# Quantised convolutions as four 64x64 tiles, with GpSimd in the quantisation: a residual chain of convolutions on one core

## The chip, the cores and the metric

One core of a Trainium2 chip runs the whole program. The metric is the device time of one execution in microseconds (us). The kernel before took 255.37 us (median of 3 runs, 255.18 to 255.53). What a profile shows is one execution, taken on its own.

## The reference

The input x is (16, 32, 28, 28) in float32. Four layers follow one another:

- Layer 0: a 1x1 convolution 32 to 192, a 3x3 convolution 192 to 192 and a 1x1 projection 192 to 32, all with ternarised weights, each with a batch norm, the first two with a clip to 0..6; then x is added.
- Layer 1: two 3x3 convolutions 32 to 32 with 8-bit quantised weights and activations. The input of each is scaled by 255 over the largest value of the **whole** tensor and rounded:

```
s = max(max(x), 1e-8) / 255;  q = clip(round(x / s), 0, 255) * s
out = relu(bn1(conv3x3(q(x), q(w1))))
out = relu(bn2(conv3x3(q(out), q(w2))) + identity)
```

- Layers 2 and 3: a 3x3 convolution 32 to 32, bias, batch norm, relu, and a channel of an image is set to zero if its largest value is under 0.001.

So layer 1 has two points at which everything waits for a maximum over all images: one ahead of each quantised convolution.

## The kernel before

**Layout.** The 16 images are taken four at a time: a chunk c (0 to 3) holds four images g in the four groups of 32 partitions, each with 32 channels, 784 pixels long. The final tensors y0, h1, yb have this layout, [128, 4, 784].

**Layer 0** runs through 16 images in `slot(c, g)` (L612 on TensorE, L937 on ScalarE, L1385 on VectorE). TensorE works as Winograd-like rows: `outer` (L561), `middle` (L550), `pair_middle` (L572), `pair_outer` (L583), and `expand_main`/`expand_rest` (L497, L514) for images further ahead. Once per chunk, in slot g = 0 of the next chunk, the 1x1 projection follows: `project(c, h)` (L594), twice, for the even and the odd rows (h = 0, 1). Each call has 8 matmuls of 128x32 tiles (128 rows, 32 columns of the array) on h2a and 8 of 64x32 tiles on h2b, whose half h lies in partitions 64h to 64h+63. VectorE reads the result in `residual(c, h)` (L1375), which adds x, writes y0 and takes the maximum. The last chunk's projection comes at the end of layer 0, and there the two halves signal apart. `expand_main(15, 0)` writes PSUM bank 6, which the projection of chunk 2 used, and so waits for `residual(2, 0)` (L508).

**Layer 1** (`step` L1553, `quant` L1561 and L1066, `qconv` L735). `step(k)` takes the maximum over all of it: VectorE reduces, TensorE spreads (`largest`, L729), VectorE reduces again and takes the reciprocal. Then, chunk by chunk: VectorE multiplies and adds a rounding constant (`quant`, L1566, into the two-buffer ra), ScalarE takes the constant off, clips at zero and casts to bf16 (L1069, into qi), TensorE does the convolution, ScalarE does relu and scale (`out1`, L1073), VectorE takes maxima (L1599). Each is cut into two halves of the rows. `qconv` uses a weight matrix wqi of 128x128 with four 32x32 blocks on its diagonal, one for each image of the chunk: 9 taps x 2 halves of 128x128 tiles, 18 matmuls a chunk, 72 for a convolution. Before the maxima and between them TensorE runs idle matmuls (`keep_warm`, L485).

After the second convolution, ScalarE has scaled and shifted the residual (`shifted`, L1091), and VectorE adds it to the result (`q_out`, L1646). Then VectorE splits the result into two float16 parts (`q_hi`, `q_lo`) and VectorE, ScalarE and DMAs copy these into stacks `kst` (`copies`, `stack`, `blocks`, `dup`) for layers 2 and 3, whose convolutions `lconv` (L758) use 128x32 tiles. The order on every engine is written out by hand: on VectorE from L1694, on TensorE from L790, on ScalarE from L1115, on the DMA queue from L401. The float16 weights of these convolutions are made on VectorE (L1575 to L1580) while the first quantised convolution runs; L1584 to L1589 are five small scalars beside it. GpSimd has only the set-up and, at the very end, three output scalings (L464).

Of the kernel before, what the change touches and what calls it, by code (L numbers as in the profile page):

```python
# [134 lines left out]
def conv_seq(nc, x, params, w1, w2a, w2b, w3, wq1, wq2, wc, wd, out):  # L135
    with ExitStack() as ctx:
# [322 lines left out]


# [7 lines left out]
        def _(pe):  # L468
# [125 lines left out]
            def project(c, h, steps=(0, 1, 2, 3), bank=7, end=False):  # L594

                if bank == 6 and not end:
                    pe.wait_ge(ra_ready, 2 * (G * (c + 1) + 2) + 2)
                wait(pe, y0_ready, (2 * c + h if end else 2 * c) if bank == 7 else 0)
                lower = slice(HB * h, HB * h + HB)
                for s in steps:  # L600
                    if s == 0:
                        pe.wait_ge(h2a_ready, (c + 1) * G + (h if end else 0))
                    if s == (2 if end else 1):
                        pe.wait_ge(h2_ready, (c + 1) * G)
                    for g in range(G):
                        w, rhs = ((w3t[:, 0, :], h2a[:, g, s, HALF * h:HALF * h + HALF]) if s < 2 else
                                  (w3t[lower, 1, :], h2b[lower, g, s - 2, :]))
                        i = nc.tensor.matmul(ps[C * g:C * g + C, bank, :HALF], w, rhs, start=(s == steps[0]),  # L608
                                             stop=(s == steps[-1]))
# [1179 lines left out]
```

## Time and profile before

| | |
|---|---|
| profiled execution | 254.96 us |
| its span, first to last instruction | 253.2 us |
| PE busy | 230.3 us (91%) |
| DVE (VectorE) busy | 226.3 us (89%) |
| ACT (ScalarE) busy | 178.6 us (71%) |
| POOL (GpSimd) busy | 8.7 us (3%) |
| mean granted TensorE clock | 0.999 |

Engine times are unions of the instructions of one engine; waiting is not in them. A matmul is shown with some 0.33 us although a new one can start 0.17 us after the last, so that a busy PE can hide small pauses. "idle before" is the engine's idle time, with the instruction that ended it.

### The profile page before, as it was taken

What the parts mean: (1) busy time and instruction counts of PE and PEld (TensorE: products, weight loads), DVE (VectorE), ACT (ScalarE), POOL (GpSimd) and SP (SyncE); (2) the same over time, 40 slices, a digit from 0 to 9 for tenths busy, and PEclk for the clock granted to TensorE, in tenths of its full rate; (3) what the DMA queues carried; (4) which work ended last, traced back from release to release, by engine and by line L of the source; (5) the groups of instructions that cost most, each with busy time, mean ns of one, the idle gap of its engine ahead of it and who ended that gap; (6) DMA issues with size and microseconds to landing.
All of it is one profiled execution on the core that took longest, in us unless ns stands there. A gap on an engine that the chain in (4) does not pass through costs nothing.

```text
span 253.2 us, 5577 instructions
## 1 busy us (share of the span) xinstructions
PE 230.3 (91%) x2151; PEld 132.2 (52%) x2151; DVE 226.3 (89%) x460; ACT 178.6 (71%) x268; POOL 8.7 (3%) x26
## 2 busy tenths in 40 slices
PE   0659998999999999999999999999979999789991
PEld 0315564556555555555555555465525555446551
DVE  3799999999999999999999997879777769999894
ACT  5899987885684586776376479683525739997963
POOL 4500000000000000000000000000000000000013
PEclk9999999999999999999999999999999999999999
DMA  7427202111003202003202001100000000264206
GB/s 234 119 58 242 61 1 70 28 28 38 0 21 84 58 3 63 1 3 87 74 0 57 11 0 34 32 3 0 3 1 1 3 0 12 54 153 104 61 20 254
DMA packets 9018, 13.13 MB, mean 52 GB/s; under 512 B 2560, under 2 KB 7136, under 8 KB 8992
## 3 DMA queue, kind: packets, MB, share of 16 engines
q1 hardware_dynamic: 8800, 12.74, 18.8%
q8 instruction: 17, 0.28, 0.5%
q14 instruction: 9, 0.07, 0.1%
q10 hardware_dynamic: 192, 0.04, 0.1%
HBM read 4.04 MB, written 1.61 MB: 22 GB/s over the span
## 4 chain that ended last, share of the span: by engine, by line
PE 68%; DVE 13%; DMA 5%; ACT 5%; SPq 3%; issue 3%; DVEq 0%; ACTq 0%
PE ps L556 17%; PE ps L567 17%; PE ps L589 10%; PE ps L578 8%; PE ps L742 5%; PE ps L608 2%; DMA big<-w2b_in 2%; PE ps L780 2%; PE ps L511 2%; SPq L390 2%; PE ps L677 2%; DVE big L1644 2%; DVE cmx L1689 2%; DMA big<-big 1%; DVE vv L1651 1%
## 5 line engine op out<-in xcount | busy, mean ns | idle before, releaser
L567 PE MATMUL ps<-vv,w2at 128*128 128x378 f16 (+1 forms) x192 | 37.2, 330 | 0.4 <-DVE ps L1330 0.4
L861 ACT ACTIVATE ra<-ps,bn 128x392 f32<-128x392 f32 x32 | 21.4, 676 | 22.9 <-PE ps L511 22.3
L556 PE MATMUL ps<-vv,wu 128*128 128x392 f16 x180 | 34.8, 329 | 0.1
L780 PE MATMUL ps<-big,wst 128*32 128x378 f16 (+10 forms) x576 | 24.5, 326 | 3.6 <-DVE big L1644 2.4
L567 PEld LDWEIGHTS ps<-vv,w2at 128*128 128x128 f16 x192 | 17.8, 98 | 15.3 <-issue 4.3
L742 PE MATMUL ps<-qi,wqi 128*128 128x378 bf16 (+7 forms) x144 | 23.9, 325 | 0.6 <-ACT qi L1069 0.6
L556 PEld LDWEIGHTS ps<-vv,wu 128*128 128x128 f16 x180 | 17.4, 98 | 12.1 <-DVE vv L1313 0.5
L780 PEld LDWEIGHTS ps<-big,wst 128*32 128x32 f16 x576 | 15.2, 96 | 13.0 <-issue 2.2
L567 PE MATMUL ps<-vv,w2bt 128*128 128x378 f16 (+1 forms) x96 | 21.2, 330 | 0.0
L556 PE MATMUL ps<-vv,wub 128*128 128x378 f16 (+1 forms) x90 | 19.9, 330 | 0.0
L742 PEld LDWEIGHTS ps<-qi,wqi 128*128 128x128 bf16 x144 | 13.8, 97 | 10.8 <-ACT qi L1069 1.4
L589 PE MATMUL ps<-vv,w2at 128*64 128x378 f16 (+1 forms) x192 | 19.0, 333 | 0.0
L893 ACT ACTIVATE hs<-ug,magic 128x784 f16<-128x784 f16 x16 | 15.1, 946 | 5.2 <-DVE ug L1273 5.1
L578 PE MATMUL ps<-vv,wu 128*64 128x378 f16 (+1 forms) x192 | 18.7, 330 | 0.0
L1330 DVE SCALAR_TENSOR_TENSOR ps<-ps,c1a 128x392 f32<-128x392 f32 x32 | 16.6, 563 | 2.3 <-ACT c1a L877 2.3
L913 ACT ACTIVATE r2a<-ps,bn 128x784 f32<-128x784 f32 x15 | 15.0, 1002 | 5.1 <-DVE h2a L1351 5.0
L870 ACT ACTIVATE ra<-ps,bn 128x392 f32<-128x392 f32 x18 | 12.0, 677 | 8.3 <-PE ps L526 8.3
L1100 ACT COPY big<-part 32x784 f16<-32x784 f16 x20 | 16.9, 843 | 1.0 <-DVE part L1683 0.7
L1287 DVE SCALAR_TENSOR_TENSOR hs<-ra,hs 128x784 f16<-128x784 f32 x16 | 15.4, 965 | 0.0
L1069 ACT ACTIVATE qi<-ra,magic 128x420 bf16<-128x420 f32 (+1 forms) x16 | 9.0, 611 | 9.0 <-DVE ra L1566 9.0
L1351 DVE SCALAR_TENSOR_TENSOR h2a<-r2a,h2a 128x784 f16<-128x784 f32 x15 | 14.5, 968 | 0.1
L589 PEld LDWEIGHTS ps<-vv,w2at 128*64 128x64 f16 x192 | 9.7, 109 | 8.1 <-issue 4.5
(220 smaller groups left out, 436.9 us busy)
## 6 DMA issues: line engine op xcount, KB each, us to landing
xk<-xpart SPq DMA_DIRECT2D x45, 49.0 KB, 1.9
xin<-x_in SPq DMA_DIRECT2D x4, 392.0 KB, 3.8
big<-part SPq DMA_DIRECT2D x25, 49.0 KB, 2.0
hs<-ug SPq DMA_DIRECT2D x12, 98.0 KB, 2.2
hs<-lowp SPq DMA_DIRECT2D x12, 98.0 KB, 2.2
big<-big SPq DMA_DIRECT2D x3, 392.0 KB, 3.6
y_out<-xin SPq DMA_DIRECT2D x3, 392.0 KB, 2.4
big<-w2a_in SPq DMA_DIRECT2D x3, 288.0 KB, 4.4
```

What stands on the lines that cost most here:

```text
L556: i = nc.tensor.matmul(landing(slice(0, P), PBANK[k], dx), weights(raw, mid, k, dx, False), moving(s, k, dx, b), start=(n == 0 and dx == D ...
L567: i = nc.tensor.matmul(landing(slice(0, P), PBANK[k], dx), weights(raw, mid, k, dx, False), moving(s, k, dx, b), start=False, stop=(n == 2 ...
L578: i = nc.tensor.matmul(landing(slice(HB * q, HB * q + HB), 4, dx), weights(raw, mid, k, dx, True), moving(s, k, dx, b), start=(n == 0 and ...
L589: i = nc.tensor.matmul(landing(slice(HB * q, HB * q + HB), bank, dx), weights(raw, mid, k, dx, True), moving(s, k, dx, b), start=False, st ...
L742: i = nc.tensor.matmul(img(ps[:, bank + h, :W * rows], rows)[:, to[0], to[1]], wqi[:, k, t, :], qi[:, c, of[0], of[1]], start=(t == TAP_OR ...
L780: i = nc.tensor.matmul(img(ps[C * g:C * g + C, bank + h, :W * n], n)[:, to[0], to[1]], wst[:, layer, C * t:C * t + C], kst[:, KBUF[layer][ ...
L861: nc.scalar.activation(ra[:, 0, HALF * h:HALF * h + HALF], ps[:, bank, :HALF], ACT.Relu, bias=bn[:, BSH, BN1A:BN1A + 1], scale=bn[:, BSC, ...
L893: nc.scalar.activation(rows_of(hs[:, MAIN_HI]), img(ug[:, 0, :]), ACT.Identity, bias=magic[:, 2:3]).then_inc(hha_ready, 1)
L913: nc.scalar.activation(img(r2a[:], 2), ps[:, 0:2, :HALF], ACT.Relu, bias=bn[:, BSH, BN2A:BN2A + 1], scale=bn[:, BSC, BN2A:BN2A + 1]).then_ ...
L1100: ins = nc.scalar.copy(kst[C * k:C * k + C, KBUF[layer][c], g], part[C * g:C * g + C, layer, c % 2, k])
L1287: stt(rows_of(hs[:, MAIN_LO]), img(ra[:, 0, :]), CAP, rows_of(hs[:, MAIN_HI]), ALU.min, ALU.subtract).then_inc(hla_ready, 1)
L1330: stt(ps[:, k, :HALF], ps[:, PBANK[2], :HALF], half, c1a[:], ALU.mult, ALU.add).then_inc(seed_a, 1)
```

## The change

- `qconv` no longer uses 128x128 tiles with a block diagonal of four images, but 64x64 tiles with a diagonal of two (wqi is half as wide). For each tap there are four matmuls: a pair of images (partitions 0 to 63, 64 to 127) by a half of the rows. Convolution 1 reads the pair from its partitions and writes the half `to` into partitions 64*half, so its output h1 has the half of the rows where the pair of images was, and the pair along the free axis. Convolution 2 reads that layout and writes the usual one. It needs a row of the other half at the seam, so its input is a new tile qh with a row above and below each half.
- The second step of the quantisation goes from ScalarE to GpSimd: `quant` for the first convolution, `quant_halves` for the second; ScalarE copies only the seam rows of qh (two small operations a chunk). `qconv` waits for both halves of a chunk. `shifted` goes to GpSimd as well, in a written order.
- `out1` is one ScalarE operation a chunk (two for the last), and one maximum each instead of two.
- `project` is one call for both halves: first the 128x32 tiles of both, then the 64x32 tiles of both, alternating between the upper and lower 64 rows of the array. It signals once, at its end, in the last chunk too.
- VectorE makes the weights of the later convolutions in the slots of the last chunk of layer 0 (`tail_weights`), and the five small scalars after them.
- On VectorE `quant(3, 1)` moves to a place between `q_hi(0)` and `q_lo(0)`. On TensorE the fourth chunk of convolution 2 moves ahead of `lconv(0, 0)`.

```diff
-            def project(c, h, steps=(0, 1, 2, 3), bank=7, end=False):
+            def project(c, banks, end=False):
...
+                wait(pe, y0_ready, 2 * c)
+                for h in range(2):
+                    pe.wait_ge(h2a_ready, (c + 1) * G + (h if end else 0))
+                    for s in range(2):
+                        for g in range(G):
+                            nc.tensor.matmul(ps[C * g:C * g + C, banks[h], :HALF], w3t[:, 0, :],
+                                             h2a[:, g, s, HALF * h:HALF * h + HALF], start=(s == 0), stop=False)
+                pe.wait_ge(h2_ready, (c + 1) * G)
+                for s in range(2):
+                    for k in range(G):
+                        for h in range(2):
+                            g = (k + 2 * h) % G
+                            lower = slice(HB * h, HB * h + HB)
+                            i = nc.tensor.matmul(ps[C * g:C * g + C, banks[h], :HALF], w3t[lower, 1, :],
+                                                 h2b[lower, g, s, :], start=False, stop=(s == 1))
                 i.then_inc(proj_done, 1)
...
             def qconv(k, c, bank, done):
...
+                for t in TAP_ORDER:
+                    for n in range(4):
+                        pair, half = n // 2, (n // 2 + n) % 2
+                        of, to = (pair, half) if k == 0 else (half, pair)
+                        out_, in_ = tap_window(t, HALF_ROWS * half, HALF_ROWS)
+                        lanes = slice(HB * of, HB * of + HB)
+                        if k == 0:
+                            moving_ = qi[lanes, c, in_[0], in_[1]]
+                        else:
+                            top = HALF_ROWS * half - 1
+                            moving_ = qh[lanes, c, pair, in_[0].start - top:in_[0].stop - top, in_[1]]
+                        i = nc.tensor.matmul(img(ps[HB * to:HB * to + HB, bank + of, :HALF], HALF_ROWS)[:, out_[0], out_[1]],
+                                             wqi[lanes, k, t, :], moving_, start=(t == TAP_ORDER[0]),
                                              stop=(t == TAP_ORDER[-1]))
-                    i.then_inc(done, 1)
+                i.then_inc(done, 1)
...
             for c in range(NCH):
-                wait(pe, h1_ready, 2 * (c - 1))
+                wait(pe, h1_ready, c - 1)
+                pe.wait_ge(q_ready, 2 * c + 2)
                 qconv(0, c, 2 * (c % 2), q1_done)
...
             def qconv2(c):
-                wait(pe, t1_ready, c - 1)
-                qconv(1, c, QBANK[c % 2], q2_done)
+                pe.wait_ge(qh_ready, c + 1)
+                pe.wait_ge(qm_ready, 2 * c + 2)
+                qconv(1, c, QBANK[c], q2_done)
```

On GpSimd:

```diff
+            def quant(c):
+                for h, rows in enumerate((slice(0, HALF_ROWS + 1), slice(HALF_ROWS + 1, H))):
+                    pool.wait_ge(q_v, 2 * c + h + 1)
+                    pts(qi[:, c, rows], img(qf[:, c % 2, :])[:, rows], -MAGIC, 0.0, ALU.add, ALU.max).then_inc(q_ready, 1)
+            def quant_halves(c):
+                for r in range(2):
+                    pool.wait_ge(q_v, 2 * (NCH + c) + r + 1)
+                    pts(qh[:, c, r, 1:HALF_ROWS + 1], img(qf[:, c % 2, HALF * r:HALF * r + HALF], HALF_ROWS), -MAGIC, 0.0,
+                        ALU.add, ALU.max).then_inc(qm_ready, 1)
+            def shifted(c):
+                pool.wait_ge(scale_ready, 2)
+                pts(y0[:, c, :], y0[:, c, :], col[:, BD + 2:BD + 3], col[:, SIG + 3:SIG + 4], ALU.mult,
+                    ALU.add).then_inc(ys_ready, 1)
+            for c in range(NCH):
+                quant(c)
+            quant_halves(0)
+            quant_halves(1)
+            shifted(0)
+            quant_halves(2)
+            shifted(1)
+            quant_halves(3)
+            shifted(2)
+            shifted(3)
```

On ScalarE, and then on VectorE:

```diff
+            def quant_halves(c):
+                act.wait_ge(q_v, 2 * (NCH + c) + 2)
+                nc.scalar.activation(qh[high_, c, :, 0], by_half[low, :, HALF_ROWS - 1], ACT.Relu, bias=magic[low, 0:1])
+                nc.scalar.activation(qh[low, c, :, HALF_ROWS + 1], by_half[high_, :, 0], ACT.Relu,
+                                     bias=magic[high_, 0:1]).then_inc(qh_ready, 1)
...
+            slot(NCH - 1, 0, last=True)
+            dve.wait_ge(ws_ready, 1)
+            tail_weights(0)
+            slot(NCH - 1, 1, last=True)
+            tail_weights(1)
+            slot(NCH - 1, 2, last=True)
...
             q_out(0)
             q_hi(0)
+            quant(3, 1, h1)
             q_lo(0)
```

## Rows read from the trace of the kernel before

**Rows 1.** Windows: us, busy time of PE, PEld, DVE, ACT, POOL; clock; DMA

```profile
60.00:100.00 40.00, 40.00 (x334) 22.87 (x333) 39.20 (x71) 27.04 (x41) 0.00 (x0) 1.00 0.15 37
...
220.00:230.00 10.00, 8.84 (x162) 5.17 (x154) 9.49 (x22) 8.91 (x12) 0.00 (x0) 1.00 0.56 127
...
252.00:253.20 1.20, 0.00 (x0) 0.00 (x0) 0.00 (x0) 0.00 (x0) 0.00 (x0) 0.72 0.19 72
```

**Rows 2.** Timeline, PE: projections; start, length, engine, line, tile, shape, count

```profile
159.96 0.52 PE L608 MATMUL ps<-h2a,w3t 128*32 128x392 f16 x8
160.40 0.51 PE L608 MATMUL ps<-h2b,w3t 64*32 64x392 f16 x8
...
161.74 1.17 PE L567 MATMUL ps<-vv,w2at 128*128 128x392 f16 x6
...
185.73 0.54 PE L608 MATMUL ps<-h2b,w3t 64*32 64x392 f16 x16
```

**Rows 3.** Timeline, DVE, last chunk of layer 0

```profile
161.59 0.62 DVE L1380 SCALAR_TENSOR_TENSOR y<-ps,bn,xin 128x392 f32<-128x392 f32 x1
...
170.07 1.05 DVE L1330 SCALAR_TENSOR_TENSOR ps<-ps,c1a 128x392 f32<-128x392 f32 x2 [1.00 <-ACT c1a L877]
...
180.11 0.64 DVE L1341 SCALAR_TENSOR_TENSOR ps<-ps,sgn,cy 128x392 f32<-128x392 f32 x1 [0.56 <-ACT cy L884]
```

**Rows 4.** Timeline, DVE: the weights that are moved

```profile
194.54 0.36 DVE L1577 TENSOR_SCALAR wcr<-wcr,col 128x288 f32<-128x288 f32 x1
...
195.77 0.37 DVE L1577 TENSOR_SCALAR wcr<-wcr,col 128x288 f32<-128x288 f32 x1
```

**Rows 5.** Timeline: end of layer 0

```profile
186.50 0.57 DVE L1363 SCALAR_TENSOR_TENSOR h2a<-r2a,h2a 128x392 f16<-128x392 f32 x1
...
187.26 0.63 DVE L1380 SCALAR_TENSOR_TENSOR y<-ps,bn,xin 128x392 f32<-128x392 f32 x1
```

**Rows 6.** Timeline: first quantised convolution

```profile
189.65 0.16 DVE L1555 TENSOR_REDUCE mx<-cmx 128x1 f32<-128x9 f32 x1
...
191.17 1.43 DVE L1566 TENSOR_SCALAR ra<-y,col 128x420 f32<-128x420 f32 x4
191.64 2.19 ACT L1069 ACTIVATE qi<-ra,magic 128x420 bf16<-128x420 f32 x4 [5.57 <-DVE ra L1566]
...
192.34 7.96 PE L742 MATMUL ps<-qi,wqi 128*128 128x392 bf16 x48 [0.27 <-ACT qi L1069]
```

**Rows 7.** Timeline: its end and the second maximum

```profile
201.31 0.68 ACT L1075 ACTIVATE h2a<-ps,bn,col 128x392 f32<-128x392 f32 x1 [0.66 <-PE ps L742]
202.02 0.56 DVE L1599 TENSOR_REDUCE cmx<-h2a 128x1 f32<-128x392 f32 x1 [0.78 <-ACT h2a L1075]
...
205.33 0.16 DVE L1555 TENSOR_REDUCE mx<-cmx 128x1 f32<-128x9 f32 x1
```

**Rows 8.** Groups by form, POOL: busy us, mean ns of one

```profile
L464 POOL TENSOR_SCALAR xin<-vv,keep 128x784 f32<-128x784 f32 x3 | 2.8, 918 | 236.4 <-DVE keep L1691 236.4
...
L455 POOL TENSOR_SCALAR bn<-bn 128x4 f32<-128x4 f32 x1 | 0.3, 254 | 0.1
```

**Rows 9.** Timeline: second quantisation up to the residual

```profile
208.91 1.41 DVE L1566 TENSOR_SCALAR ra<-h2a,col 128x420 f32<-128x420 f32 x4
...
211.54 1.03 DVE L1651 SCALAR_TENSOR_TENSOR vv<-ps,col,y 128x784 f32<-128x784 f32 x1 [0.25 <-ACT y L1092]
```

**Rows 10.** Timeline: two operations at one time in the set-up

```profile
7.24 0.96 DVE L1203 TENSOR_TENSOR xpart<-xrest 128x784 bf16<-128x784 f32 x1
7.77 0.49 POOL L449 TENSOR_TENSOR bn<-bn,par 128x9 f32<-128x9 f32 x1
...
8.61 0.20 POOL L453 TENSOR_TENSOR bn<-par,bn 128x9 f32<-128x9 f32 x1
```

**Rows 11.** Timeline, PE, after the second quantised convolution

```profile
218.41 3.10 PE L780 MATMUL ps<-big,wst 128*32 128x392 f16 x72 [1.46 <-DVE big L1644]
...
225.62 12.40 PE L780 MATMUL ps<-big,wst 128*32 128x392 f16 x288 [1.08 <-DMA big<-big]
```

More of the change, by code:

```diff
@@ L592, in pair_outer @@
                 i.then_inc(convb_done, 1)
-            def project(c, h, steps=(0, 1, 2, 3), bank=7, end=False):
-                if bank == 6 and not end:
+            def project(c, banks, end=False):
+                if not end:
                     pe.wait_ge(ra_ready, 2 * (G * (c + 1) + 2) + 2)
[L598 to L609, printed above, removed]
+                wait(pe, y0_ready, 2 * c)
[13 more added lines that the diff above has]
+                                                 h2b[lower, g, s, :], start=False, stop=(s == 1))
                 i.then_inc(proj_done, 1)
@@ L725, in _ @@
             pe.wait_ge(ra_ready, 2 * B)
-            project(NCH - 1, 0, end=True)
-            project(NCH - 1, 1, (2, 3, 0, 1), bank=6, end=True)
+            project(NCH - 1, (7, 6), end=True)
             def largest(n):
@@ L1076, in out1 @@
+            def out1(c):
+                act.wait_ge(q1_done, c + 1)
+                pieces = 1 if c < NCH - 1 else 2
+                for h in range(pieces):
+                    r = slice(h, h + 1) if pieces == 2 else slice(0, 2)
+                    bank = 2 * (c % 2)
+                    nc.scalar.activation(img(h1[:, c, :], 2)[:, r], ps[:, bank:bank + 2, :HALF][:, r], ACT.Relu,
                                          bias=bn[:, BSH, BNQ1:BNQ1 + 1],
                                          scale=col[:, SIG:SIG + 1]).then_inc(h1_ready, 1)
-            quant(0, 0)
@@ L1080, in _ @@
             act.wait_ge(scale_ready, 1)
-            for c in range(1, NCH):
-                quant(c, 0)
-                out1(c - 1)
-            out1(NCH - 1)
-            act.wait_ge(q1_done, 2 * NCH)
-            for c in range(2):
-                quant(c, 1)
-            act.wait_ge(scale_ready, 2)
-            def shifted(c):
-                nc.scalar.activation(y0[:, c, :], y0[:, c, :], ACT.Identity, bias=col[:, SIG + 3:SIG + 4],
-                                     scale=col[:, BD + 2:BD + 3]).then_inc(ys_ready, 1)
+            for c in range(NCH):
+                out1(c)
@@ L1095, in stack @@
+            for c in range(NCH):
+                quant_halves(c)
             def stack(layer, c):
@@ L1561, in quant @@
             def quant(c, k, src):
-                wait(dve, q_ready, 2 * (NCH * k + c - 1))
-                for px in (slice(0, HALF + W), slice(HALF + W, HW)):
+                if k and c >= 2:
+                    dve.wait_ge(qh_ready, c - 1)
+                    dve.wait_ge(qm_ready, 2 * (c - 1))
+                else:
+                    wait(dve, q_ready, 2 * (NCH * k + c - 1))
+                split = HALF if k else HALF + W
+                for px in (slice(0, split), slice(split, HW)):
                     ts(qf[:, c % 2, px], src[:, c, px], c1(RS + k), MAGIC, ALU.mult, ALU.add).then_inc(q_v, 1)
@@ L1614, in _ @@
             quant(1, 1, h1)
-            for c in range(2, NCH):
-                quant(c, 1, h1)
+            quant(2, 1, h1)
             def halves_l(layer, c):
```

98 lines of the change are left out of this document (37 added, 61 removed).

## The prediction

> **What bounds the kernel now.** Read the windows first. In layer 0 TensorE is busy all 40.00 of 40 us while VectorE has 39.20; in the last part (220 to 230 us) VectorE has 9.49 of 10 us and TensorE 8.84 [rows 1]. So there are three regimes: layer 0 goes by TensorE, with VectorE close behind; the two maxima of layer 1 are a chain in which each engine waits for the next; the splitting and stacking afterwards goes by VectorE. Then the timeline, engine by engine, at the places the diff touches: what a freed engine is worth depends on the regime.
>
> I write "before" for the profiled execution: 254.96 us, span 253.2. It lies 0.4 us under the median of 255.37, which I add at the end.
>
> **Projections in layer 0.** The two calls start at 159.96 and the next work at 161.74: 1.78 us. The step from one shape of tile to another is visible: 0.44 us from 159.96 to 160.40 for two passes of 0.17, thus 0.1 more [rows 2]. Can 64-row tiles in the upper and lower half run at one time? At 185.73, 16 matmuls of 64x32 took 0.54 us where 8 took 0.51: yes [rows 2]. The new order has four passes of 128x32 and two of eight 64x32 tiles, with two changes of shape: 6 x 0.17 + 2 x 0.1 = 1.2 us. 0.57 us less for each of three projections. For chunks 0 and 1 that is 1.1 us on the engine that bounds; bounds: 0, if VectorE (39.20 of 40) can't follow, and 1.7 with the third.
>
> **Weights moved into the last chunk.** One `tail_weights` takes 1.2 us of VectorE (start to start, 194.54 to 195.77) [rows 4]. The first delays `residual(2, 0)` from 161.59 to 162.8, done 163.45. TensorE needs bank 6 of it for `expand_main(15, 0)`, nine matmuls after 161.74, that is at 163.24, and with the faster projection at 162.67: it now waits, the third gain is gone and 0.2 us more. VectorE then idles 1.0 us ahead of L1330 at 170.07 and 0.56 us ahead of 180.11 [rows 3], which hides most of both; the second one and the five scalars (0.7 us, at 0.15 each from start to start) come through with some 0.3 us. I take +0.5; bounds -0.6 (all hidden, third gain kept) and +1.9 (nothing of 2.5 us hidden but the 0.57).
>
> **Last projection.** Before, `residual(3, 0)` started 0.76 us after L1363 started and waited for no matmul [rows 5]. Now it waits for the common signal: L1363 ends at 187.07, then two passes of 128x32, a change, two of 64x32 and 0.33 us of latency: about 188.1 instead of 187.26: +0.8. Bounds +0.3 and +1.0.
>
> **First quantised convolution**, from L1555 to the next L1555: before 205.33 - 189.65 = 15.7 us [rows 6, 7]. GpSimd's price: 918 ns for 784 elements and 254 for 4 [rows 8] make 0.25 us + 0.85 ns an element: 0.61 and 0.56 us for the two halves, 1.17 a chunk. ScalarE needed 2.19 us for four, 1.10 a chunk [rows 6], so the rate is no loss. But the convolution now waits for both halves: VectorE's first at 191.17, GpSimd from +0.57 (0.47 was ScalarE's, 0.1 is my guess for GpSimd's later start) to +1.74, TensorE at +1.8 instead of +1.17.
> Then the matmuls: 48 in 7.96 us, so 0.162 us each, 2.92 a chunk [rows 6]. Four 64x64 tiles at one time need nine passes: 1.46. TensorE chunks start at +1.8, 3.3, 4.7, 6.2, and the last ends at +7.8; GpSimd delivers at +1.7, 2.9, 4.1, 5.25, always in time. After that two ScalarE operations of 0.68 and a maximum of 0.56 [rows 7] put L1555 at +9.7. From L1555 to L1555: 1.52 + 9.7 = 11.2 us, a gain of 4.5, if GpSimd and VectorE don't touch each other.
>
> **Do they?** In the set-up a GpSimd operation on 128x9 took 0.49 us beside a two-input VectorE operation and ended 0.06 us after it; the like, alone, took 0.20 [rows 10]. So one row says that GpSimd waits for VectorE. The multiplications L1566 (four of 420 elements in 1.43 us, under 1 ns an element, so two elements at a time [rows 6]) are followed at once by GpSimd. If each GpSimd operation and each VectorE operation take turns, eight of 0.585 and eight of 0.35 make 7.5 us, TensorE's last chunk starts at +7.5 instead of +6.2, and the gain is 3.2. An operation has a dispatch part that needs no memory, so turns cost less than their sum; I take half: gain 3.9. Bounds: 4.5 and, if the tiles don't overlap, a loss of 1.3 (below).
>
> The Trainium skill (SBUF — State Buffer, "Who interferes with whom") speaks against the change: VectorE in a two-port mode or with two SBUF inputs and GpSimd hold the shared port pair exclusively, and "the other fully blocks". Row and rule agree for the wait of GpSimd; no row here shows VectorE held up by GpSimd. By the rule in both directions the result is the second case below.
>
> **Second quantisation.** Before, from L1555 to `q_out(0)` 6.2 us [rows 7, 9], held by ScalarE's `shifted(0)`. Now GpSimd does quant_halves(0), then (1), which has to wait for the second multiplication, 208.91 - 205.33 = 3.6 us after L1555 [rows 7, 9], and then `shifted(0)`: 3.6 + 0.57 + 1.17 + 0.92 = 6.3. So the double speed of TensorE buys nothing here: the wait is for the residual as before. With turns between the engines +0.5; bounds 0.06 and +2.0 (small scalars of VectorE held up by two GpSimd operations, 1.1, and three later turns). ScalarE's seams (two operations, under 0.55 each) lie beside GpSimd's 1.17.
>
> **After that** VectorE has no pause, and its work is the same, except that `quant(3, 1)`, which stood in the wait for `shifted(0)`, stands now between q_hi and q_lo: +0.7 (half of 1.41 [rows 9]). `shifted(1)` can be late for `q_out(1)`: +0.3; bounds 0 and +2.7 (after `shifted(0)` GpSimd has four operations of 0.58 and three of 0.92, 5.1 us, and about half of that can meet q_hi, quant(3), q_lo and the copies). ScalarE loses some 8 us of work here, worth nothing: VectorE bounds.
>
> **Sum:** -1.1 + 0.5 + 0.8 - 3.9 + 0.5 + 0.7 + 0.3 = -2.2. 254.96 - 2.2 = 252.8, and 0.4 to the median: **253.2 us**.
>
> **The rivals.**
> 1. *No conflict at all:* -1.1 + 0.5 + 0.8 - 4.5 + 0.1 + 0.7 = -3.5: 251.9 us. For it: the GpSimd operations at the end took 918 ns beside VectorE maxima, but those read a single input. It belongs to my forecast's own range, 251.5 to 254.6.
> 2. *Exclusive in both directions (the slower side).* VectorE's multiplications, scalars, q_hi, q_lo and copies wait for whole GpSimd operations: -1.1 + 0.5 + 0.8 - 3.2 + 2.0 + 0.7 + 2.7 = +2.4: 257.8 us. It decides once VectorE loses over 2.2 us after the second maximum, beyond the forecast. For it rows 10; against it that a small wait of GpSimd was seen, none of VectorE.
> 3. *The tiles don't overlap as 64x64.* Then the first stage has 4 x 2.92 behind +1.8, ends its last maximum at +15.5, 17.0 in all, +1.3 instead of -3.9; sum +3.0: 258.4. Against it: both kinds of overlap exist in the trace, column tiles (72 in 3.10 us [rows 11]) and row tiles [rows 2].
> 4. *The clock falls.* TensorE's fourth chunk used to lie in the pause between 221.5 and 225.62 [rows 11]; now the pause is empty, 4.1 us. At the end TensorE stops at 248.1, and in 252.0 to 253.2 the granted clock is 0.72 [rows 1]: full until about 252.5, so 4.4 us after the last matmul it fell to half (1.2 GHz). If it falls here, the 3.1 us of `lconv(0, 1)` and part of the next take twice as long and VectorE waits for the result: +2: 255.2.
>
> **Chances.** Forecast with rival 1: 0.55 (of it 0.15 near 252). Rival 2: 0.24. Rival 3: 0.06. Rival 4: 0.15, half of it inside "same", the rest on both sides. A measurement of this kernel tells 0.2%, 0.5 us, from no change: faster means under 254.9, slower over 255.9. Faster 0.60, same 0.12, slower 0.28. Range 251.3 to 257.7, which leaves out half of rival 2's upper side and rival 3.
>
> **What would show it.** L742's successor at 36 matmuls in about 1.5 us a chunk (rival 3: 2.9). Mean duration of the GpSimd operations: 0.58 and 0.61 if free, more if they wait; multiplications at 0.35 or stretched; q_lo at 0.97 or more. L1555 to its successor: 11.2 to 12.5 us. `q_out(0)` released by GpSimd. Granted clock in the pause before `lconv(0, 1)`. The projection at 1.2 us. The forecast is wrong if VectorE's operations beside GpSimd are stretched by over 2 us in all, or if layer 0 ends later than before.

## The result, and the profile after

The changed kernel takes **264.76 us** (median of 4 runs, 264.63 to 267.21) against 255.31 us (4 runs, 255.18 to 255.53): ratio 1.0388, 95% interval 1.0361 to 1.0416. The forecast was 253.2, its range ended at 257.7. The profiled execution took 264.63 us, its span is 262.8. Of the page, busy times and the chain that ended last:

```profile
PE 224.3 (85%) x2295; PEld 130.4 (50%) x2295; DVE 228.9 (87%) x457; ACT 168.2 (64%) x253; POOL 38.3 (15%) x47
...
PE 52%; DVE 19%; POOL 10%; ACT 8%; issue 5%; DMA 3%; SPq 2%; DVEq 0%; ACTq 0%
```

VectorE's 226.3 us became 228.9, TensorE's 230.3 became 224.3, ScalarE lost 10.4; GpSimd went from 8.7 to 38.3 us, and it is a tenth of the chain. The windows show where (columns as in [rows 1]):

```profile
190.00:200.00 10.00, 6.94 (x84) 3.96 (x84) 5.34 (x18) 1.00 (x1) 8.00 (x6) 0.83 0.00 0
...
210.00:220.00 10.00, 6.15 (x73) 3.72 (x72) 6.29 (x19) 2.16 (x7) 10.00 (x7) 0.66 0.01 2
220.00:230.00 10.00, 6.54 (x116) 4.27 (x120) 8.64 (x12) 4.76 (x7) 7.65 (x6) 0.83 0.16 42
```

In 210 to 220 us GpSimd (the last of the five engines in a row) is busy all ten microseconds, the other three stand idle for part of them (TensorE has 6.15, VectorE 6.29, ScalarE 2.16), and the granted clock is 0.66. GpSimd's groups by form (busy us, mean ns):

```profile
L470 POOL TENSOR_SCALAR qh<-ra 128x392 bf16<-128x392 f32 x8 | 13.0, 1647 | 5.7 <-DVE ra L1616 5.7
L464 POOL TENSOR_SCALAR qi<-ra 128x420 bf16<-128x420 f32 x4 | 6.5, 1638 | 182.2 <-DVE ra L1616 182.2
L464 POOL TENSOR_SCALAR qi<-ra 128x364 bf16<-128x364 f32 x4 | 5.7, 1420 | 0.0
L476 POOL TENSOR_SCALAR y<-y,col 128x784 f32<-128x784 f32 x4 | 5.0, 1247 | 0.0
```

The quantisation takes 1.42 to 1.65 us where I had put 0.56 to 0.61. In the first stage TensorE does its chunks quickly and waits for them (timeline, PE; what answers to [rows 6] on L742). The first row holds two chunks, with the granted clock at 0.50 in 196 to 198 us:

```profile
195.18 4.82 PE L779 MATMUL ps<-qi,wqi 64*64 64x392 bf16 x72 [2.80 <-POOL qi L464]
201.21 1.66 PE L779 MATMUL ps<-qi,wqi 64*64 64x392 bf16 x36 [1.21 <-POOL qi L464]
204.18 1.66 PE L779 MATMUL ps<-qi,wqi 64*64 64x392 bf16 x36 [1.31 <-POOL qi L464]
```

On VectorE (what answers to [rows 6, 7, 9]) the two maxima, `q_out(0)` and what follows it:

```profile
189.96 0.16 DVE L1601 TENSOR_REDUCE mx<-cmx 128x1 f32<-128x9 f32 x1
...
207.76 0.16 DVE L1601 TENSOR_REDUCE mx<-cmx 128x1 f32<-128x9 f32 x1
...
217.12 1.03 DVE L1683 SCALAR_TENSOR_TENSOR vv<-ps,col,y 128x784 f32<-128x784 f32 x1 [3.03 <-POOL y L476]
218.19 0.73 DVE L1689 TENSOR_SCALAR part<-vv 128x784 f16<-128x784 f32 x1
218.84 0.99 DVE L1616 TENSOR_SCALAR ra<-h2a,col 128x392 f32<-128x392 f32 x2
...
220.76 1.05 DVE L1663 COPY big<-part 32x784 f16<-32x784 f16 x1
...
226.77 1.03 DVE L1683 SCALAR_TENSOR_TENSOR vv<-ps,col,y 128x784 f32<-128x784 f32 x1 [0.97 <-POOL y L476]
```

These starts cut any variant of the kernel into four stretches. The table has them for all, each from its own timeline; "before" is the kernel before, "after" the changed one. A row is one execution: that of 7 is the fastest of its ten (255.31 us, median 257.77), that of 12 the slowest of its five (253.30, median 252.20).

| span in us | to max 1 | max 1 to max 2 | max 2 to q_out(0) | q_out(0) to end | span |
|---|---|---|---|---|---|
| before | 189.65 | 15.68 | 6.22 | 41.62 | 253.2 |
| after | 189.96 | 17.80 | 9.36 | 45.72 | 262.8 |
| 1 quantisation on ScalarE | 190.07 | 12.55 | 7.06 | 44.72 | 254.4 |
| 2 the same, idle matmuls | 189.82 | 12.55 | 7.06 | 43.09 | 252.5 |
| 3 before, quantisation on GpSimd | 189.91 | 18.78 | 9.10 | 41.86 | 259.6 |
| 4 before, new projection | 189.30 | 15.68 | 6.23 | 41.60 | 252.8 |
| 5 fast form in conv 2 only | 190.64 | 17.81 | 7.02 | 47.10 | 262.6 |
| 6 the same, idle matmuls | 190.08 | 17.81 | 7.02 | 43.86 | 258.8 |
| 7 add,mult everywhere, no clip | 189.66 | 11.26 | 7.03 | 45.56 | 253.5 |
| 8 steps exchanged, idle matmuls | 190.14 | 12.06 | 7.13 | 43.27 | 252.6 |
| 9 as 2, residual on GpSimd | 189.83 | 12.55 | 5.52 | 44.05 | 252.0 |
| 10 as 9, quant(3, 1) later | 190.00 | 12.55 | 5.52 | 43.64 | 251.7 |
| 11 as 10, gated | 189.84 | 12.55 | 5.52 | 43.64 | 251.5 |
| 12 as 11, fewer idle matmuls | 191.14 | 12.55 | 5.52 | 42.29 | 251.5 |

The first column doesn't tell small differences: variants with the changed kernel's layer 0 have 189.66 to 191.14 there, and the kernel before has 189.65 here and 190.30 and 191.08 in the executions of the two benches.

### The profile page after: what moved, and what is told of

Read it like the earlier page. It is cut to its first block, busy times and chain, and to the rows that moved or that the text cites. A ratio compares the mean times of both kernels' runs of the same rounds, so it can differ in the third digit from the quotient of the medians.

```text
span 262.8 us, 5871 instructions
## 1 busy us (share of the span) xinstructions
PE 224.3 (85%) x2295; PEld 130.4 (50%) x2295; DVE 228.9 (87%) x457; ACT 168.2 (64%) x253; POOL 38.3 (15%) x47
## 4 chain that ended last, share of the span: by engine, by line
PE 52%; DVE 19%; POOL 10%; ACT 8%; issue 5%; DMA 3%; SPq 2%; DVEq 0%; ACTq 0%
PE ps L596 14%; PE ps L585 13%; PE ps L607 7%; PE ps L618 7%; POOL qh L470 5%; POOL qi L464 5%; DMA big<-w2b_in 2%; PE ps L540 2%; PE ps L708 2%; PE ps L779 2%; PE ps L818 2%; DVE cmx L1721 1%; ACT big L1134 1%; PE ps L725 1%; DVE big L1676 1%
## 5 line engine op out<-in xcount | busy, mean ns | idle before, releaser
L464 POOL TENSOR_SCALAR qi<-ra 128x420 bf16<-128x420 f32 (+1 forms) x8 | 12.0, 1529 | 182.2 <-DVE ra L1616 182.2
L818 PE MATMUL ps<-big,wst 128*32 128x378 f16 (+10 forms) x576 | 25.2, 333 | 5.2 <-DMA big<-big 4.4
L585 PEld LDWEIGHTS ps<-vv,wu 128*128 128x128 f16 x180 | 17.4, 98 | 11.8 <-DVE vv L1342 0.2
L779 PE MATMUL ps<-qh,wqi 64*64 64x378 bf16 (+2 forms) x144 | 10.1, 447 | 7.3 <-POOL qh L470 7.3
L1145 ACT ACTIVATE vv<-ps,bn,col 128x392 f32<-128x392 f32 (+2 forms) x16 | 10.3, 676 | 9.3 <-PE ps L818 9.2
L1119 ACT ACTIVATE h2a<-ps,bn,col 128x784 f32<-128x784 f32 (+1 forms) x5 | 4.3, 872 | 17.4 <-PE ps L779 17.4
```

Source lines behind the costliest of these rows:

```text
L464: pts(qi[:, c, rows], img(qf[:, c % 2, :])[:, rows], -MAGIC, 0.0, ALU.add, ALU.max).then_inc(q_ready, 1)
L585: i = nc.tensor.matmul(landing(slice(0, P), PBANK[k], dx), weights(raw, mid, k, dx, False), moving(s, k, dx, b), start=(n == 0 and dx == D ...
L779: i = nc.tensor.matmul(img(ps[HB * to:HB * to + HB, bank + of, :HALF], HALF_ROWS)[:, out_[0], out_[1]], wqi[lanes, k, t, :], moving_, star ...
L818: i = nc.tensor.matmul(img(ps[C * g:C * g + C, bank + h, :W * n], n)[:, to[0], to[1]], wst[:, layer, C * t:C * t + C], kst[:, KBUF[layer][ ...
```

## The experiments

"x us beside y" gives the medians of the variant and of the kernel before, measured together; then come their ratio and its 95% interval.

**What a GpSimd operation costs by its form.** My theory after the result: the form `add, max` is slow. Rivals: the bf16 output, or VectorE beside it.

```diff
  (in words) forms on GpSimd at the end of the kernel before, then four times more beside VectorE operations
+ (qd, src, -MAGIC, 0.0, ALU.add, ALU.max), (y0, ...same), (qd, src, -MAGIC, 1.0, ALU.add, ALU.mult), (y0, ...same),
+ (y0, src, 1.0, 1.0, ALU.mult, ALU.mult), (qd, src, -MAGIC, ALU.add), (qd, src, 0.0, ALU.max), (784: mult, add by columns)
```

> The kernel before, and after its last computation GpSimd runs eight forms of tensor_scalar one after another, first with VectorE idle, then four times more beside VectorE operations: 14 multiplications of 784 float32 (two elements at a time), 14 additions with two SBUF inputs, 14 maxima, 14 float16 copies. The extra work changes no output. In the changed kernel GpSimd's operation on 392 elements took 1.51 us where I had 0.58. Theory 1 (the form): the operation with a maximum in it is slow by itself: 1.5 us with VectorE idle, while mult,mult and add,mult on the same 392 elements take about 0.6, whatever the output type. Theory 2 (the output type): bf16 output is what is slow; then add,mult into bf16 takes 1.5 and add,max into float32 0.6. Theory 3 (contention): with VectorE idle all forms take about 0.6 and only beside the multiplications, additions and copies 1.5. In all of them the residual form (mult,add with two column scalars, 784 elements) should take 0.95 alone and up to 1.7 beside two-port or two-input VectorE work, but not beside maxima.

Timeline, POOL, with VectorE idle: add,max into bf16, into float32; add,mult into bf16; add alone; mult,add on 784:

```profile
250.93 1.56 POOL L487 TENSOR_SCALAR qi<-ra 128x392 bf16<-128x392 f32 x1 [1.00 <-ACT xin L1163]
252.58 1.52 POOL L487 TENSOR_SCALAR y<-ra 128x392 f32<-128x392 f32 x1
254.18 0.52 POOL L487 TENSOR_SCALAR qi<-ra 128x392 bf16<-128x392 f32 x1
...
255.98 1.20 POOL L487 TENSOR_SCALAR qi<-ra 128x392 bf16<-128x392 f32 x1
...
258.55 0.99 POOL L487 TENSOR_SCALAR y<-ra,col 128x784 f32<-128x784 f32 x1
```

Beside single-input float32 operations of VectorE the first and the third of them:

```profile
259.91 2.15 POOL L487 TENSOR_SCALAR qi<-ra 128x392 bf16<-128x392 f32 x1 [0.21 <-DVE cmx L1772]
...
264.31 0.71 POOL L487 TENSOR_SCALAR qi<-ra 128x392 bf16<-128x392 f32 x1
```

The form decides, a factor of three; the output type doesn't matter. VectorE beside it costs 0.2 to 0.6 us on top, and is itself stretched: 0.57 to 0.75 us where one alone takes 0.56. VectorE's rows beside that first one:

```profile
259.74 0.56 DVE L1775 TENSOR_SCALAR r2a<-ra 128x784 f32<-128x784 f32 x1 [9.17 <-issue]
...
260.34 2.92 DVE L1775 TENSOR_SCALAR r2a<-ra 128x784 f32<-128x784 f32 x4
```

Beside VectorE additions with two SBUF inputs `add, max` took 2.22, `add, mult` 1.12 and the scaling of 784 elements 1.78 instead of 0.99. Beside VectorE reductions neither engine changed (1.53 and 0.97), beside float16 copies only VectorE did (0.36 to 0.56). A second bench asked which operation is slow; I had come to it by experiment 5 below, where `add, add` was slow too.

```diff
  (in words) the forms of the first bench exchanged for others
- add,max; add,mult; mult,mult; add; max; on 784: mult,add
+ add,add; add,mult; mult,add; mult,max; max,mult; mult; on 784: add,max; add,mult
```

> The kernel before with eight more GpSimd operations appended at its end (its total time means nothing), once with VectorE idle and once beside single-input VectorE operations. Single arithmetic forms on 128x392 float32 into bf16: add,add; add,mult; mult,add; mult,max; max,mult; mult alone; and on 128x784 into float32 add,max and add,mult. If a multiplication among the two operations makes the form fast (theory F), then add,add takes about 1.5 us, mult alone, add,mult, mult,add, mult,max and max,mult all about 0.52, and at 784 elements add,max about 2.7 and add,mult about 1.0. If max is slow in itself beside add,add (theory G), mult,max and max,mult take 1.2 us or more. If a single operation is slow whatever it is, mult alone takes 1.2 us.

The first five in this order, and `add, max` on 784 elements:

```profile
251.70 1.55 POOL L487 TENSOR_SCALAR qi<-ra 128x392 bf16<-128x392 f32 x1 [1.00 <-ACT xin L1163]
253.34 0.52 POOL L487 TENSOR_SCALAR qi<-ra 128x392 bf16<-128x392 f32 x1
253.94 0.52 POOL L487 TENSOR_SCALAR qi<-ra 128x392 bf16<-128x392 f32 x1
254.54 1.55 POOL L487 TENSOR_SCALAR qi<-ra 128x392 bf16<-128x392 f32 x1
256.17 1.53 POOL L487 TENSOR_SCALAR qi<-ra 128x392 bf16<-128x392 f32 x1
...
259.07 2.84 POOL L487 TENSOR_SCALAR y<-ra 128x784 f32<-128x784 f32 x1
```

Neither theory holds in full: a multiplication alone took 1.20, and one paired with a maximum 1.53 to 1.55. Fast were only the pairs add,mult, mult,add and mult,mult; the rest took 1.20 to 1.56 us, the pair add,max 3.4 ns an element ((2.84 - 1.52)/392, both into float32).

**The complement: everything but GpSimd (1), and GpSimd alone (3).**

```diff
 1, on ScalarE instead of GpSimd, in the new layout
+ nc.scalar.activation(qi[:, c, rows], ..., ACT.Relu, bias=magic[:, 0:1]).then_inc(q_ready, 1)   # and qh, and the residual
 3, in the kernel before: its quantisation's second step only
+ pts(qi[:, c, rows], ..., -MAGIC, 0.0, ALU.add, ALU.max).then_inc(q_ready, 1)
```

> The changed kernel with everything kept (64x64 tiles, new projection, moved weights) except that both quantisation steps' second half and the residual scaling are back on ScalarE, GpSimd has none of it. If the loss of 9.4 us is GpSimd's price: maximum to maximum (L1601) about 12 us instead of 17.8 (ScalarE's 1.10 a chunk against TensorE's 1.5), the residual q_out(0) some 6.3 us after the second maximum instead of 9.4, no GpSimd conflict later: 252 to 254 us, faster than before. Rival: the loss comes from the tiles and orders (ScalarE now carries quantisation, relu, seams; the clock falls in TensorE's pauses): 258 us or more.

> The kernel before with only the second quantisation step (L1069) of both convolutions on GpSimd; tiles of 128x128, residual on ScalarE, old projection. GpSimd needs 1.6 + 1.42 = 3.0 us a chunk where ScalarE took 1.1 and TensorE 2.9. If the price of GpSimd's form is the cause: first stage 1.1 us later start and GpSimd-bound at 3.0 a chunk: about +1.5 us from maximum to maximum; second stage +1.1 and no more, as the later chunks lie beside VectorE's work: 257.5 to 259 us. If contention on VectorE is the main cause, VectorE's multiplications, q_hi, q_lo and copies stretch by 0.3 to 0.7 each: 260 or more.

1: 256.72 us beside 255.71, ratio 1.0061 (1.0033 to 1.0088). 3: 261.63 beside 255.71, 1.0235 (1.0206 to 1.0264). GpSimd alone (3) loses 3.1 and 2.9 us in the two middle stretches; the tiles without it (1) gain 3.1 in the first of these. 3 came out above its 257.5 to 259 us, where "260 or more" had been contention's. Its trace doesn't show contention as the cause: GpSimd works 12.37 us without a pause (191.96 to 204.33), 1.55 an operation as alone, the last chunk's matmuls can start only then (204.47), and later `q_hi(0)` and `q_lo(0)` have their usual 0.57 and 0.98 us. 1 missed its 252 to 254 us: it is slower than before at its end. Timeline, PE, 1:

```profile
217.91 4.78 PE L788 MATMUL ps<-big,wst 128*32 128x392 f16 x72 [2.08 <-DVE big L1668]
```

The same 72 matmuls took 3.10 us before [rows 11]; the granted clock was 0.92 in 210 to 220 us and 0.74 in the next ten.

**The projection alone (4)**, for the first term of the sum.

```diff
 the kernel before, with
- project(c - 1, 0, bank=6)
- project(c - 1, 1)
+ project(c - 1, (6, 7))
```

> The kernel before with only the new projection, in the last chunk too. Theory: three times -0.57 us on TensorE in layer 0, as no weights are moved there, and +0.8 at the end, where the first residual waits for the common signal (measured in the changed kernel: 187.57 - 187.07 rather less, +0.6): sum -0.9 to -1.1, so 254.3 us. Rival: VectorE can't follow the faster TensorE, the gain is zero and only the wait is left: +0.6, 255.9.

254.60 us beside 255.71, 0.996 (0.9943 to 0.9977): a gain, without anything else of the change.

**The form in place (5), the clock held (2, 6).** In 5, ahead of the first convolution VectorE scales and clips (mult,max) and GpSimd rounds with `add, add`; ahead of the second VectorE is as it was and GpSimd does `add, mult`. In 2 and 6 idle matmuls stand in TensorE's pauses of the second stage; the granted clock is 1.00 from the second maximum to 240 us in both.

```diff
 5
- -MAGIC, 0.0, ALU.add, ALU.max
+ MAGIC, -MAGIC, ALU.add, ALU.add      # conv 1
+ -MAGIC, 1.0, ALU.add, ALU.mult       # conv 2
 2 and 6 (shortened)
+ qconv2(0); idle(3); qconv2(1); idle(6); qconv2(2); idle(6); qconv2(3); idle(10); lconv(0, 0); idle(14)
```

> The version with quantisation and residual on ScalarE, and only idle matmuls added on TensorE in its pauses of the second stage: 3, 6 and 6 between the four chunks, 10 ahead of lconv(0, 0), 14 (2.3 us) between it and lconv(0, 1). They change no output. In that version the granted clock was 0.74 in 220 to 230 us and lconv(0, 0) took 4.78 us instead of 3.10. Theory (the clock): with the pauses filled the clock stays at 1.00, lconv(0, 0) takes 3.1 us, and the part behind q_out(0) shrinks from 44.7 us to about 42 (before: 41.7): 253.5 to 254.5 us. Rival (the orders): the part behind q_out(0) is longer because quant(3, 1) and ScalarE's seams stand in the way; then the time stays within 0.5 us of 256.7, or grows because the idle matmuls delay the real ones.

> The changed kernel, with only the forms of GpSimd's quantisation exchanged for ones without a maximum: first convolution VectorE mult,max and GpSimd add,add (rounding constant on and off); second convolution VectorE as it was and GpSimd add,mult by 1. The results are the same numbers. Theory (the form is the price): each GpSimd operation falls from 1.4-1.6 us to 0.5-0.75, maximum to maximum from 17.8 to about 12.3 us, q_out(0) from 9.4 to about 6.5 us after the second maximum; the clock still falls in TensorE's pause as in the ScalarE version: 255.5 to 257.5 us in all, against 264.8. Rival (contention with VectorE is the price): the operations stay over 1.0 us and the time over 260.

> The fast forms and the idle matmuls together. If form and clock are the two causes of the whole loss, this is what was forecast for the change: 252.5 to 254 us. If something else of the change costs (the common signal of the last projection, the moved weights, contention), it stays at 255 or more.

2: 254.97 beside 255.17, 0.999 (0.9971 to 1.0008). 5: 264.44 beside 255.17, 1.0327 (1.0265 to 1.0389). 6: 260.78, 1.021 (1.0185 to 1.0236). Nothing in 5's first stretch moved, since `add, add` is no faster; with `add, mult` the wait for `q_out(0)` fell from 9.36 to 7.02. 5 and 6 missed what was expected of them by 7 us, because of `add, add`. The clock's price is what the idle matmuls give back: 3.7 us from 5 to 6, 1.8 from 1 to 2 (0.7% of 255).

**The decisive pair (7, 8).** 7 leaves out the clip at zero, so negative inputs of the first convolution go through and its output is not the reference's: it prices the form and is no version to keep. 8 leaves nothing out. It has the same number of operations on GpSimd, with the two steps exchanged between the engines, the order of VectorE's scalars changed to suit, and idle matmuls almost as in 2 (4 where that has 6).

```diff
 7, the changed kernel with
- -MAGIC, 0.0, ALU.add, ALU.max
+ -MAGIC, 1.0, ALU.add, ALU.mult
 8, GpSimd does the first step, VectorE the second
+ pts(qf[:, c % 2, px], y0[:, c, px], col[:, 38:39], MAGIC, ALU.mult, ALU.add).then_inc(q_v, 1)
+ ts(qi[:, c, rows], img(qf[:, c % 2, :])[:, rows], -MAGIC, 0.0, ALU.add, ALU.max).then_inc(q_ready, 1)
```

> The changed kernel with one thing exchanged: both quantisation steps on GpSimd are add,mult (-MAGIC, 1.0) instead of add,max (-MAGIC, 0.0), so the clip of negative inputs in the first convolution is left out; engines, tiles, order and waits are as in the changed kernel. If the form is the cause (theory F), the operations fall to 0.5 to 0.7 us, maximum to maximum falls from 17.80 to 11.8 to 12.6 us, q_out(0) stands 7.0 us after the second maximum instead of 9.36, and the time is about 264.8 - 5.4 - 2.3 = 257 plus what the falling clock still takes in the tail (up to 2): 257 to 259. If it is GpSimd beside VectorE and TensorE (contention, theory C), maximum to maximum stays over 15 us and the time over 261.

> The changed kernel with the two steps of the quantisation exchanged between the engines, nothing left out: GpSimd does the first one (mult by the scale, add MAGIC), VectorE the second (add -MAGIC, max 0, into bf16); idle matmuls hold the clock in the second stage. GpSimd has as many operations as in the changed kernel, in another form. Theory F: GpSimd's are 0.55 us for 420 elements, maximum to maximum 12.0 to 13 us (17.80 in the changed kernel), time 254.5 to 257. Theory C: over 15 us and over 259.

7: 257.77 us beside 255.48, 1.0065 (1.0037 to 1.0094). 8: 254.76, 0.9978 (0.9965 to 0.9991). GpSimd's groups and TensorE's timeline, 7:

```profile
L464 POOL TENSOR_SCALAR qi<-ra 128x420 bf16<-128x420 f32 x4 | 2.5, 628 | 181.9 <-DVE ra L1616 181.9
L464 POOL TENSOR_SCALAR qi<-ra 128x364 bf16<-128x364 f32 x4 | 2.5, 613 | 0.0
```

```profile
192.96 6.04 PE L779 MATMUL ps<-qi,wqi 64*64 64x392 bf16 x144 [0.88 <-POOL qi L464]
```

With engines, tiles, order and waits as in the changed kernel, the first stretch falls from 17.80 to 11.26 us. The form of GpSimd's quantising instructions is the cause of that, and of 7.0 us of the 9.5 in all (264.76 to 257.77). VectorE pays a little: the first convolution's eight multiplications took 0.57 us each instead of 0.44 and 0.40 (420 and 364 elements), and scalars beside GpSimd took 0.47 instead of 0.15. And 7 is still slower than the kernel before, 8 only 0.2% faster: with the right form the change as it stands is worth about nothing.

**The rest of the tail (9 to 12).** With the clock held the last stretch is still 1.5 to 2.4 us longer than before. 9 puts the residual scaling alone on GpSimd; 10 moves `quant(3, 1)` behind `copies(0, 0)` and the fourth chunk behind `lconv(0, 0)`, with 20 idle matmuls ahead of `lconv(0, 0)` instead of 10 and 6 behind the fourth chunk instead of 14 behind `lconv(0, 0)`; 11 lets the third scaling wait for `copies(0, 0)` and the fourth for `dup(0, 0)`; 12 cuts 20 idle matmuls to 8.

```diff
 10 (on VectorE)
+ q_hi(0); q_lo(0); copies(0, 0); quant(3, 1, h1)
 11 (on GpSimd)
+ if c == 2: pool.wait_ge(stack_v[0], 1)
+ elif c == 3: pool.wait_ge(v_dup, 1)
 12 (on TensorE, ahead of lconv(0, 0))
- idle(20, 2)
+ idle(8, 2)
```

> As the last, and the residual's scaling (the cheap form mult,add, 0.99 us alone for 784 elements) on GpSimd, the quantisation still on ScalarE. ScalarE had it behind quant_halves(0) and (1), so q_out(0) came 7.06 us after the second maximum. On GpSimd it can start with scale_ready, so q_out(0) waits for the first chunk of the convolution: about 5.6 us after the maximum, and 1.0 to 1.5 us less in all: 252 to 253 us. Rival: GpSimd's four operations meet q_hi, q_lo and the copies of VectorE and cost what they save: same as the version with all on ScalarE.

> The variant with the quantisation on ScalarE, the residual shift on GpSimd and idle matmuls (254.15 us beside 255.17), with quant(3, 1) placed behind copies(0, 0) on VectorE, and its ScalarE half and the fourth chunk of the convolution behind stack(0, 0) and lconv(0, 0). There quant(3, 1) stood between q_hi(0) and q_lo(0) and took 1.33 us beside GpSimd, and q_lo(0) ended 4.3 us after q_out(0) began, against 2.65 in the kernel before. If this chain sets the tail, lconv(0, 0) starts 7.4 to 8 us after q_out(0) instead of 9.2, and the time is 252.5 to 253.5; if the later quant(3, 1) makes q_out(3) or the next copies late, or VectorE's total work bounds anyhow, it stays at 254.1.

> The kernel with quant(3, 1) behind copies(0, 0) (253.78 us beside 255.48), where GpSimd's four residual scalings ran in one go from 206.33 to 211.25 and VectorE's q_hi(0) took 1.25 us and q_lo(0) 1.65 beside them, against 0.57 and 0.97 in the kernel before. Now the third scaling waits for copies(0, 0) and the fourth for dup(0, 0). Theory C (GpSimd beside these operations stretches them): q_hi(0) about 0.6 and q_lo(0) about 1.0, the first later convolution starts 7.8 us after q_out(0) instead of 9.17, and the time is 252.4 to 253.0. Rival: the stretch has another cause, or the wait goes on elsewhere: q_hi(0) and q_lo(0) stay over 1.1 and 1.5, or the time stays at 253.5 or more.

> The kernel with the gated residual scalings (253.77 us beside 255.37), with 8 idle matmuls instead of 20 ahead of the first later convolution. Its trace showed q_hi(0) and q_lo(0) back at 0.57 and 0.98 us, and yet the convolution started 9.17 us after q_out(0): the 26 idle matmuls ran to 217.08, while dup(0, 0), which it needs, ended at 215.30. If the idle matmuls are what held it, it starts 7.5 to 7.7 us after q_out(0), VectorE's waits of 0.28 and 0.89 us for the first layer-2 results go, and the time is 252.2 to 253.0. If the tail is bounded otherwise, or the clock falls in the shorter cover, it stays within 0.4 us of 253.8.

9: 254.15 beside 255.17, 0.9955 (0.9939 to 0.9971). 10: 253.78 beside 255.48, 0.994 (0.9923 to 0.9956). 11: 253.77 beside 255.37, 0.9942 (0.9925 to 0.996). 12: **252.20** beside 255.17, **0.9883** (0.9862 to 0.9905). Of these only 12 met its expected time. 9 has `q_out(0)` 5.52 us after the maximum, as expected, but loses part of that again to stretched VectorE operations; in 10 and 11 the first later convolution started 9.17 us after `q_out(0)`, against 9.20 in 9. `q_hi(0)` and `q_lo(0)` in 10, beside GpSimd:

```profile
209.14 1.25 DVE L1695 TENSOR_SCALAR part<-vv 128x784 f16<-128x784 f32 x1
210.43 1.65 DVE L1700 SCALAR_TENSOR_TENSOR part<-vv,part 128x784 f16<-128x784 f32 x1
```

The same in 11, and its TensorE:

```profile
208.98 0.57 DVE L1699 TENSOR_SCALAR part<-vv 128x784 f16<-128x784 f32 x1
209.58 0.98 DVE L1704 SCALAR_TENSOR_TENSOR part<-vv,part 128x784 f16<-128x784 f32 x1
...
214.33 0.97 DVE L1686 COPY big<-big 64x3136 f16<-64x3136 f16 x1
```

```profile
212.66 4.49 PE L810 MATMUL ps<-w2at 128*128 128x392 f16 x26
217.08 3.10 PE L797 MATMUL ps<-big,wst 128*32 128x392 f16 x72
```

The gate took 1.35 us of stretch off VectorE and won nothing, for my idle matmuls ran to 217.08 though the convolution's input was ready at 215.30. In 12 it starts 7.54 us after `q_out(0)` instead of 9.17. Two more runs have `quant(3, 1)` behind `dup(0, 0)`, the first beside 11, the second beside 12.

> The same, and quant(3, 1) comes behind dup(0, 0) on VectorE, its ScalarE part behind stack(0, 1). If its 0.76 us ahead of dup(0, 0) still holds up the first later convolution, that starts 7.0 us after q_out(0) (6.86 in the kernel before), and the time is 251.6 to 252.4. If VectorE's total work after q_out(0) bounds the tail, the time is that of the kernel without this move within 0.3 us.

> The same with quant(3, 1) behind dup(0, 0), and 6 idle matmuls there (254.03 us with 20). If both held the convolution, it starts 6.8 to 7.0 us after q_out(0), as in the kernel before (6.86), and the time is 251.6 to 252.6; if VectorE's work bounds, it equals the other variant of this pair within 0.3 us.

254.03 beside 255.37 (0.9944, 0.9927 to 0.996) and 252.82 beside 255.17 (0.9898, 0.9879 to 0.9916). In the second the convolution starts at 6.87, as in the kernel before, and that buys nothing over 12 (the intervals overlap): the start of the first later convolution no longer bounds.

## Why the prediction was wrong

**The step that failed** is "GpSimd's price". I took a line through `mult, mult` on 784 elements and a 4-element operation [rows 8] and read it as the price of GpSimd's tensor_scalar; the change issues `add, max`. 0.61 and 0.56 us were 1.64 and 1.42. With it fell the next sentence, that ScalarE's rate makes this "no loss": 3.0 us a chunk against ScalarE's 1.10 and TensorE's 1.46.

Term by term, in the profiled executions (+9.7 us where the sum had -2.2):

- *Layer 0* (-1.1 + 0.5 + 0.8 = +0.2): +0.31, but the same layer 0 varied by 1.5 us between executions, so that the sum proves little and the parts must do. The third gain went as said: TensorE waits for `residual(2, 0)`. At the end L1392 (L1363 before), which the last projection waits for, starts at 185.90 instead of 186.50, and the residual 1.67 us after it instead of 0.76: +0.9 for the +0.8 (PE and DVE, after):

```profile
162.50 0.34 PE L540 MATMUL ps<-xk,w1t 96*128 96x392 bf16 x1 [0.64 <-DVE y L1409]
```

```profile
187.57 0.63 DVE L1409 SCALAR_TENSOR_TENSOR y<-ps,bn,xin 128x392 f32<-128x392 f32 x1 [0.83 <-PE ps L640]
```

  Experiment 4 has the new call at 159.25 to 160.48, 1.23 us for 1.2.
- *First convolution* (-3.9): +2.1. Its other parts were right: 36 matmuls in 1.46 to 1.49 us from start to start, and with the fast form (7) the working without conflict (11.2) meets 11.26. The half I added for turns (11.8) was too much here. The 0.35 us of the multiplications, which I read as four of 420 elements, is the distance from start to start of two of 420 and two of 364; they last 0.44 and 0.40.
- *To `q_out(0)`* (+0.5): +3.1. The order of waits was right: it waits for GpSimd's residual, as rows of after show. But the four halves ahead of that residual took 6.31 us instead of 2.3 (POOL, after):

```profile
209.72 6.31 POOL L470 TENSOR_SCALAR qh<-ra 128x392 bf16<-128x392 f32 x4 [5.69 <-DVE ra L1616]
```

  Of the 3.1 the form is 2.3 (9.36 against 7.03 in experiment 7).
- *Tail* (+0.7 + 0.3): +4.1. The first thing is GpSimd's price again, by a path that the prediction didn't look at: behind `q_out(0)` it asked only when the residuals come and what VectorE loses. From 209.72 to 225 us the chain that ended last lies on GpSimd alone, and `q_out(0)` is not in it (start, length, what; the last two rows are the fourth chunk and `lconv(0, 0)`):

```profile
209.72 6.31 POOL qh L470 x4
216.03 0.99 POOL y L476
217.02 3.28 POOL qh L470 x2
220.30 1.30 POOL y L476
221.60 3.39 POOL qh L470 x2
...
225.12 2.37 PE ps L779 x30
227.49 3.98 PE ps L818 x70
```

  The change had moved the fourth chunk ahead of `lconv(0, 0)` on TensorE, so that this waited for GpSimd's last halves too. It starts 10.31 us after `q_out(0)` instead of 6.87; its own input was there at 225.80 (DVE, after):

```profile
224.82 0.98 DVE L1676 COPY big<-big 64x3136 f16<-64x3136 f16 x1
```

  Next the clock: I had it as rival 4 with 0.15, in one place. The granted clock was 0.50 (1.2 GHz) in 196 to 198, 213 to 219 and 226 to 229 us, each time in or behind a pause of 2.8 to 3.1 us in which TensorE waited for GpSimd. In the trace after:

```profile
225.12 2.38 PE L779 MATMUL ps<-qh,wqi 64*64 64x392 bf16 x36 [3.02 <-POOL qh L470]
227.43 4.01 PE L818 MATMUL ps<-big,wst 128*32 128x392 f16 x72
```

  These took 1.66 and 3.10 us at full clock. Then `quant(3, 1)`, 0.99 for 0.7; `q_out(2)` waits 0.97 for a residual; and VectorE is stretched: `q_hi(0)` 0.73 for 0.57, the copy L1663 1.05 for 0.36. How the 4.1 us divide can't be read from after itself. By the variants the clock is worth 3.2 us in this stretch (5 against 6) and 1.6 (1 against 2). The 2.4 us that 9 has left with the clock held fell to 0.7 in 12, when the stretching of `q_hi(0)` and `q_lo(0)`, the place of `quant(3, 1)` and my own surplus of idle matmuls were gone; I have not priced these three apart, since the idle matmuls masked the first two.

The right price alone would not have saved the forecast. With the fast form (7) the median is 257.77, still 0.65% above the kernel before; with the steps exchanged and the clock held (8) it is 254.76, 0.7 us under the kernel before, where the sum had 2.2. Stretch by stretch 8 has +0.5 for the sum's +0.2, -3.6 for -3.9, +0.9 for +0.5 and +1.7 for +1.0.

**The rivals.** 1 (no conflict) describes the first stretch once the form is right. 2 (exclusive both ways) is half right: both engines were stretched, but within one GpSimd operation of 2.15 us, from 259.91 to 262.06, VectorE began three of its own, of 0.57 to 0.75 us. A lock over whole instructions doesn't give that. Here the rule of the Trainium skill (SBUF — State Buffer, "Who interferes with whom") that the loser "fully blocks" goes further than the runs. 3 (tiles don't overlap) is false. 4 was real: 1.8 us in one pair of variants, as I had priced it (+2), and 3.7 in the other. None of them was what happened: I asked what GpSimd does to its neighbours, not what its own instruction costs.

The Trainium skill (GPSIMD Engine Reference, 4.1 Engine selection) calls one-input work on GpSimd "roughly line-rate". For add,mult the benches don't speak against it (0.52 us for 392 elements, 0.85 for 784, so 0.8 ns an element); add,max took 1.52 and 2.84 us, four times as long for each element more.

## What to carry to other kernels

Price an operation moved to another engine by a row of the same form, down to its two arithmetic operations; where the trace has none, keep a wide upper bound (here other forms cost about three times the one that I had a row for). If a rounding with a clip is to be split between them, give GpSimd the multiplication with the addition and VectorE the maximum (8). A speed-up that leaves TensorE pauses gives some of it back through the clock; idle matmuls return it, but count them against the wait that they cover, since the last of them delays what comes next (11, 12). The version to keep is 12: new tiles and projection, quantisation on ScalarE, residual on GpSimd, few idle matmuls.

## What the hardware showed that I had not expected

- GpSimd's tensor_scalar on 128x392 float32: 0.52 us for add,mult, mult,add, mult,mult; 1.52 to 1.56 for add,max, add,add, mult,max, max,mult; 1.20 for one operation alone, mult too.
- GpSimd scalings of 784 elements (1.23 us each in a row of four, 0.99 alone) went with `q_lo`, with two inputs, at 1.65 us instead of 0.98 and `q_hi` at 1.25 instead of 0.57 (10); moved out of their way (11) both were back. `q_out`, which reads PSUM, stayed at 1.03.
- In the trace after TensorE waited for GpSimd for 3.08 us ahead of 213.21. The granted clock was 1.00 in 211 to 212, 0.62 in 212 to 213 and 0.50, which is 1.2 GHz, in 213 to 219 us, though TensorE worked from 213.21 on.
